# A fused attention and mixture-of-experts layer on eight cores: two instruction groups of the output-projection phase change places, and a norm's scale is computed in fewer steps

## What is computed

```python
x = x + attn(layernorm(x, eps=1e-5))            # 16 heads of 128, latent 512, S = 2048, H = 2048
x = x + ffn(layernorm(x, eps=1e-5))

def ffn(x):                                     # 8 experts, 2 of them per token, and a shared one
    h = x * rsqrt(mean(x*x) + 1e-6) * rms_weight
    probs = softmax(h @ router_w); topv, topi = top_k(probs, 2); topv /= sum(topv)
    w_dense = scatter(topi, topv)               # [tokens, 8]
    moe = sum_e w_dense[:, e] * ((silu(h @ w_gate[e]) * (h @ w_up[e])) @ w_down[e])
    return moe + (silu(h @ sw_gate) * (h @ sw_up)) @ sw_down
```

## Time and profile before

| | us |
|---|---|
| median of 2 runs | 3339.89 (3316.72 and 3363.05) |
| the profiled execution, its own time | 3065.16 |
| its span on the slowest core (core 6) | 3063.6 |
| spans of the 8 cores | 3030.8 to 3063.6 |
| mean granted TensorE clock of the 8 cores | 0.892 to 0.896 |
| output projection to router (`pb`), by the timeline | about 1045 to 1407 |
| experts (`pc`), by the timeline | about 1407 to the end |

### The profile page before, as it was taken

How to read it: one execution, slowest core, us unless ns; L and a number is a source line. 1 busy time by engine, 2 the same in 40 slices (tenths; PEclk the granted TensorE clock), 3 DMA queues, 4 the chain that set the end, 5 groups by cost and what they waited for, 6 DMA issues and landing times.

```text
span 3063.6 us, 29988 instructions; the slowest of 8 cores (3030.8 to 3063.6 us)
## 1 busy us (share of the span) xinstructions
PE 2322.3 (76%) x11593; PEld 1054.0 (34%) x11818; DVE 775.3 (25%) x1473; ACT 597.5 (20%) x905; POOL 102.6 (3%) x202
## 2 busy tenths in 40 slices
PE   0356647757777545555999999999999999999996
PEld 0122212114444322222444444444444444444443
DVE  5455362131111122111121221212122121212102
ACT  1332334217777311121000000000000000000000
POOL 1000000000000000000000000000000000000000
PEclk9977778759999767767999999999999999999998
DMA  8332000000060211016416254241634424163432
GB/s 125 136 110 69 1 0 1 0 0 1 1 111 1 84 41 42 21 35 98 71 31 105 55 84 82 46 92 28 110 55 83 83 48 90 28 110 55 83 55 110
DMA packets 48314, 182.39 MB, mean 60 GB/s; under 512 B 5656, under 2 KB 9768, under 8 KB 43056
## 3 DMA queue, kind: packets, MB, share of 16 engines
q0 software_dynamic: 40224, 130.13, 25.1%
q1 hardware_dynamic: 7952, 50.33, 4.6%
HBM read 297.93 MB, written 12.58 MB: 101 GB/s over the span
## 4 chain that ended last, share of the span: by engine, by line
PE 65%; DVE 13%; ACT 9%; issue 6%; DMA 4%; POOL 1%; DVEq 0%; ACTq 0%; SPq 0%; POOLq 0%
PE PS L1110 16%; PE PS L1064 16%; PE PS L1073 14%; ACT A_T L746 4%; PE PS L854 4%; DMA ubuf<-up_r 3%; PE PS L709 2%; DVE stats L442 2%; PE PS L609 2%; PE PS L506 2%; DVE x_lnT L484 1%; DVE ao L765 1%; ACT hT L936 1%; PE PS L737 1%; DVE sqs L638 1%
## 5 line engine op out<-in xcount | busy, mean ns | idle before, releaser
L1064 PE MATMUL PS<-hT,gbuf 128*128 128x512 bf16 x2257 | 526.4, 390 | 33.4 <-DMA ubuf<-up_r 24.5
L1110 PE MATMUL PS<-dbuf,a_fm 128*128 128x512 bf16 x2186 | 501.4, 385 | 37.6 <-DVE a_fm L1096 32.5
L1073 PE MATMUL PS<-hT,ubuf 128*128 128x512 bf16 x2186 | 490.2, 379 | 2.2
L1084 ACT ACTIVATE t1b<-PS 128x1024 f32<-128x1024 f32 x72 | 73.7, 1024 | 1472.7 <-PE PS L1078 1472.7
L1064 PEld LDWEIGHTS PS<-hT,gbuf 128*128 128x128 bf16 x2304 | 229.3, 100 | 326.6 <-issue 70.3
L1110 PEld LDWEIGHTS PS<-dbuf,a_fm 128*128 128x128 bf16 x2232 | 220.5, 99 | 308.8 <-issue 54.1
L1073 PEld LDWEIGHTS PS<-hT,ubuf 128*128 128x128 bf16 x2232 | 218.4, 98 | 263.4
L746 ACT ACTIVATE A_T<-PS,ebias 128x1024 bf16<-128x1024 f32 x256 | 272.3, 1111 | 87.1 <-PE PS L737 86.7
L1094 DVE TENSOR_TENSOR t2b<-t1b,PS 128x1024 f32<-128x1024 f32 x64 | 78.2, 1221 | 784.6 <-ACT t1b L1084 784.6
L1122 DVE TENSOR_TENSOR acc<-PS,acc 128x2048 f32<-128x2048 f32 x72 | 165.0, 2292 | 368.8 <-PE PS L1115 368.8
L709 PE MATMUL PS<-V,A_T 128*128 128x129 bf16 x1792 | 144.6, 220 | 95.3 <-ACT A_T L746 54.7
(11 more groups left out here) (201 smaller groups left out, 1414.9 us busy)
## 6 DMA issues: line engine op xcount, KB each, us to landing
gbuf<-gate_r POOLq DMA_DIRECT2D x64, 512.0 KB, 5.2
ubuf<-up_r POOLq DMA_DIRECT2D x64, 512.0 KB, 7.6
dbuf<-down_w POOLq DMA_DIRECT2D x8, 4096.0 KB, 29.4
x_in<-x_full SPq DMA_DIRECT2D x16, 1024.0 KB, 4.9
x_in<-x_own SPq DMA_DIRECT2D x8, 1024.0 KB, 5.7
WoT<-woT POOLq DMA_DIRECT2D x1, 8192.0 KB, 56.2
x_ot<-x_own SPq DMA_DIRECT2D x8, 1024.0 KB, 6.6
out<-acc SPq DMA_DIRECT2D x1, 8192.0 KB, 21.9
```

Of the source, the lines that this page charges most:

```text
L1064: e.matmul(ps_g[:, half * 512:(half + 1) * 512], gb[:, k * P:(k + 1) * P], self.hT[k][:, half * 512:(half + 1) * 512], start=(k == 0), sto ...
L1073: e.matmul(ps_g[:, 1024 + half * 512: 1024 + (half + 1) * 512], ub[:, k * P:(k + 1) * P], self.hT[k][:, half * 512:(half + 1) * 512], star ...
L1110: e.matmul(ps_d[:, nsl * 512:(nsl + 1) * 512], self.a_fm[m][:, tc * P:(tc + 1) * P], self.dbuf[:, m * H + nsl * 512: m * H + (nsl + 1) * 512],
```

## The change

Stage `a2` is cut in two. `a2` keeps the burst, the residual add and the statistics; the new `a2t` holds the scale, the shift and the writing of `h_tok`. In round `tc`, `a2(tc+1)` now stands ahead of `b1(tc)`, and `a2t(tc+1)` behind it. Only PE's list changes its order, as `b1` holds nothing but PE and ACT instructions and the ACT part of `a2` already stood behind it: PE now has the burst ahead of the transposes of `b1`. DVE and ACT keep their order, and lose the instructions named below. SP's and POOL's lists keep their order.

The waits follow: `a2(tc)` no longer waits for the evictions of `b1(tc-1)`, which now comes after it, and `b1(tc)` waits for the residual add of chunk `tc+1` (`opev[tc+1]`), since the burst has filled `PS0`.

In `a2t` both norms' scales are one: with v the variance, r = (v + 1e-5)^-0.5 and (v r^2 + 1e-6)^-0.5, the product is (v (1 + 1e-6) + 1e-11)^-0.5. It is computed as one Ln (with the bias `c_lne`) and one Exp (with the bias `c_b0`). Two ACTIVATEs and three DVE products per chunk drop out, and two memsets of 128x1 are added in `p0`.

```diff
--- before.py
+++ after.py
@@ -240,6 +240,8 @@
         self.c_pi2 = sb("c_pi2", [P, 1], F32, P0, PD)
         self.c_eps5 = sb("c_eps5", [P, 1], F32, P0, PD)
         self.c_eps6 = sb("c_eps6", [P, 1], F32, P0, PD)
+        self.c_lne = sb("c_lne", [P, 1], F32, P0, PD)
+        self.c_b0 = sb("c_b0", [P, 1], F32, P0, PD)
         self.m8 = sb("m8", [P, 8], F32, P0, PD)
         self.probs_u = sb("probs_u", [P, 8], F32, P0, PD)
         self.maskb = sb("maskb", [P, 8], F32, P0, PD)
@@ -337,6 +339,8 @@
         em(GPS, lambda e: e.memset(self.c_pi2[:, :], math.pi / 2))
         em(GPS, lambda e: e.memset(self.c_eps5[:, :], 1e-5))
         em(GPS, lambda e: e.memset(self.c_eps6[:, :], 1e-6))
+        em(GPS, lambda e: e.memset(self.c_lne[:, :], 1e-5 * 1e-6 / (1.0 + 1e-6)))
+        em(GPS, lambda e: e.memset(self.c_b0[:, :], -0.5 * math.log(1.0 + 1e-6)))
         em(GPS, lambda e: e.iota(self.rtmp[:, :], [[1, S]], base=0, channel_multiplier=0,
                                  allow_small_or_imprecise_dtypes=True))
         em(GPS, lambda e: e.iota(self.sc_c[:, :], [[1, 1]], base=0, channel_multiplier=1,
@@ -798,6 +802,7 @@
         bstage1 = {}
         bstage2 = {}
         s_h_d = {}
+        mvv = {}
         bstage = {}
 
         def stage_a1(tc):
@@ -847,7 +852,6 @@
                 wait(TEN, self.vM, aoev[tc + 1])
             if tc >= 1:
                 wait(TEN, self.vM, opev[tc - 1])
-                wait(TEN, self.sM, bstage1[tc - 1][0])
             for nsl in range(4):
                 for k in range(16):
                     em(TEN, lambda e, k=k, nsl=nsl, tc=tc:
@@ -876,22 +880,16 @@
                 self.chn(VEC, self.vM, lambda e, a0=a0, gi=gi: e.bn_stats(
                     self.stats6[:, gi * 6:(gi + 1) * 6],
                     self.acc[:, a0 + gi * 512: a0 + (gi + 1) * 512]))
-            v_mv = self.chn(VEC, self.vM, lambda e: e.bn_aggr(
+            mvv[tc] = self.chn(VEC, self.vM, lambda e: e.bn_aggr(
                 self.mv2[:, :], self.stats6[:, :].rearrange("p (g x) -> p g x", x=3)))
-            wait(SCA, self.vM, v_mv)
-            self.chn(SCA, self.sM, lambda e: e.activation(self.sc_a[:, :], self.mv2[:, 1:2], AF.Ln, bias=self.c_eps5[:, 0:1]))
-            s_r = self.chn(SCA, self.sM, lambda e: e.activation(self.sc_a[:, :], self.sc_a[:, :],
-                                                                AF.Exp, scale=-0.5))
+
+        def stage_a2t(tc):
+            a0 = tc * H
+            wait(SCA, self.vM, mvv[tc])
+            self.chn(SCA, self.sM, lambda e: e.activation(self.sc_a[:, :], self.mv2[:, 1:2], AF.Ln, bias=self.c_lne[:, 0:1]))
+            s_r = self.chn(SCA, self.sM, lambda e: e.activation(self.sc_e[:, :], self.sc_a[:, :],
+                                                                AF.Exp, scale=-0.5, bias=self.c_b0[:, 0:1]))
             wait(VEC, self.sM, s_r)
-            self.chn(VEC, self.vM, lambda e: e.tensor_mul(self.sc_c[:, :], self.sc_a[:, :], self.sc_a[:, :]))
-            v_m = self.chn(VEC, self.vM, lambda e: e.tensor_mul(self.sc_c[:, :], self.sc_c[:, :],
-                                                                self.mv2[:, 1:2]))
-            wait(SCA, self.vM, v_m)
-            self.chn(SCA, self.sM, lambda e: e.activation(self.sc_d[:, :], self.sc_c[:, :], AF.Ln, bias=self.c_eps6[:, 0:1]))
-            s_rr = self.chn(SCA, self.sM, lambda e: e.activation(self.sc_d[:, :], self.sc_d[:, :],
-                                                                 AF.Exp, scale=-0.5))
-            wait(VEC, self.sM, s_rr)
-            self.chn(VEC, self.vM, lambda e: e.tensor_mul(self.sc_e[:, :], self.sc_a[:, :], self.sc_d[:, :]))
             v_sb = self.chn(VEC, self.vM, lambda e: e.scalar_tensor_tensor(
                 self.sc_f[:, :], self.mv2[:, 0:1], -1.0, self.sc_e[:, :], ALU.mult, ALU.mult))
             wait(SCA, self.vM, v_sb)
@@ -906,9 +904,9 @@
 
         def stage_b1(tc):
             wait(TEN, self.sM, s_h_d[tc])
-            wait(TEN, self.vM, opev[tc])
-            if tc + 2 in aoev:
-                wait(TEN, self.vM, aoev[tc + 2])
+            wait(TEN, self.vM, opev[tc + 1] if tc + 1 in opev else 0)
+            if tc + 1 in aoev:
+                wait(TEN, self.vM, aoev[tc + 1])
             if tc >= 1:
                 wait(TEN, self.vM, bstage2[tc - 1][1])
                 wait(TEN, self.sM, bstage2[tc - 1][0])
@@ -981,12 +979,15 @@
         stage_a1(0)
         stage_a1(1)
         stage_a2(0)
+        stage_a2t(0)
         for tc in range(8):
             if tc + 2 < 8:
                 stage_a1(tc + 2)
+            if tc + 1 < 8:
+                stage_a2(tc + 1)
             stage_b1(tc)
             if tc + 1 < 8:
-                stage_a2(tc + 1)
+                stage_a2t(tc + 1)
             stage_b2(tc)
         self.hT_all = hT_done[7]
         self.cT_all = self.vM.n
```

## The result

| | before | after |
|---|---|---|
| median of all runs | 3063.1 us | 3022.0 us |
| median of the runs that are compared | 3061.1 us | 3019.5 us |
| ratio after to before | | 0.9864, interval 0.9849 to 0.9879 |
| profiled execution: span of the slowest core | 3063.6 us | 3020.4 us (core 5) |
| mean granted clock of the 8 cores | 0.892 to 0.896 | 0.894 to 0.902 |

The change makes the kernel 1.36% faster, 41.6 us of 3061. Forecast was a gain of 35 us and a time of 3304.9 us, between 3268 and 3342. The comparison leaves out the two runs from which the prediction took its 3339.9 us, some 9% above the other six of that kernel, and three runs of the kernel after, as long, in which the four cores of one die have a mean granted clock of 0.78 to 0.80 in place of 0.90. So the measured time, 3022.0 us, lies 246 us under the lower end of the range.

What follows compares the result with a forecast made beforehand. Rounds were bound by a chain of hand-overs, with no engine full. 7 x 4.92 = 34.4, plus 0.7 for the clock, less 0.2 for memsets, about 35 us off 3339.9: 3304.9, range 3268 to 3342.

Steps and rivals of the forecast that it cites:

- The base: Whole kernel: the gain of 35 us was taken off the median 3339.9, 275 above the profiled execution, giving 3304.9.
- The clock, ramp: Start of each burst on PE: clock at 0.50, reaching 1.00 after 5 us, taken as unchanged.
- The clock, first wave: First transposes of `b1`: may run at 2.4 GHz, gaining 0 to 0.57 us; 0.1 a round taken, 0.7 in all.
- The gap ahead of the Ln: ACT behind the evictions of `b1`: the Ln was to come 0.10 us behind the last eviction.
- The fused scale: From Ln to `h_tok`: Ln, Exp and one product take 0.95 us in place of 2.43, 1.48 less.
- The row taken for the round: One round of the earlier trace, from add to add: its links sum to 44.09 us, the whole window.
- The ends: First and last rounds: 6.75 us of `b1` moved, not saved; the gain counted as 7 x 4.92 = 34.4 us.
- A: PE's clock kept up through the shorter pause: 34 us more, 69 in all, 3271 us; chance 6%.
- B: Burst on PE never gets its clock: 90 us lost against 35 gained, 3395 us; chance 3%.
- C: Load of `ao_r` lands too late for `a1` and takes the gain back: 3340 us; chance 2%.
- D: Statistics and evictions of `b1` slow each other, only the fused scale pays: 9 us, 3331 us; chance 6%.
- E: Run spread of 1.4% hides or enlarges the gain; chance 12% over 2% faster, 4% over 2% slower, shared with other rivals.

Runs made afterwards that it cites:

- e3: The changed kernel with the transposes of `b1` also waiting for the aggregate of the statistics; ratio 0.9955 to the kernel before, round 42.32 us.
- e4: The changed kernel with four more 128x1 ACTIVATEs, one after the other, ahead of each chunk's Ln; ratio 0.9898 to the kernel before, round 39.66 us.
- e2: The kernel before with the fused scale alone, everything in its old order; ratio 0.9966 to the kernel before, round 42.67 us.
- e5: The changed kernel with 11 unread 128x512 matmuls behind the router's, while PE waits for the top two; ratio 0.9832 to the kernel before.

## Why the prediction was right and wrong

The mechanism of the gain was right: nothing overlapped in the round, the statistics went under `b1`, the experts' phase kept its length, no load came onto the path. Two numbers were wrong: the base to which the gain was applied, which put the forecast time and its whole range too high, and the size of the gain, 35 for 41, which also lies outside the 31 to 39 that the prediction gave for its mechanism alone. Link by link, for a full round, forecast and mean of 40 rounds after:

| link | forecast | after |
|---|---|---|
| add's start to `b1` | 2.72 | 2.69 |
| `b1` | 6.75 | 6.47 |
| last eviction to Ln | +0.10 | -0.16 |
| Ln to `h_tok` | 0.95 | 1.13 |
| `h_tok` to router's Exp | 2.24 | 2.24 |
| Exp to the end of the copy `cT` | 2.92 | 2.99 |
| gap and `a1` | 4.80 | 4.81 |
| gap to the burst | 0.43 | 0.43 |
| burst to the next add | 18.26 | 17.74 |
| round | 39.2 | 38.35 |

- **The base.** "The trace doesn't show where those 275 lie ... which I take to be the same there" was the step that failed: it left 275 us in the forecast time that the compared runs do not have (3061 before, 3020 after). The profiled execution, at 3065.2, was the better base: it gives 3030 for the measured 3022, and a ratio of 0.9886. That still lies just outside the interval of 0.9849 to 0.9879. The prediction saw the 9% between the profiled execution and both runs, and had no row that explained it; its range should have reached down to 3030. Its other reading of those two runs, that a change under 2% cannot be told from none, did not hold either: the interval excludes 1.
- **The clock, ramp.** "I take the ramp as unchanged": the burst is 0.46 shorter than the mean of before (18.20), and 0.52 than the one of the earlier trace rows. The largest mis-sized term. It was right that the burst does not follow the length of the pause, and wrong that the ramp is a constant: over the kernels the mean burst goes from 17.63 to 18.42, and within one from 17.05 to 18.72. That the mean of this execution fell on the short side was not foreseen, and its cause is open; this half of a microsecond a round, some 3 of the 41 us, is luck.
- **The clock, first wave.** Taken as 0.1 a round between bounds of 0 and 0.57, it gave 0.28: the wave took 0.86 on average in place of 1.14, 0.73 at best. e3 takes it away again, with the wave back at 1.14. The choice near the lower end was the error; the earlier trace rows had shown the clock at 1.00 at the very time. After the change the clock falls 2.7 to 4.4 after the add's start, and the wave starts 2.5 to 2.75 after it: where the fall comes by 2.76, the wave takes 1.14, and where it comes after 3.2, 0.73 to 0.74. Before the change it fell, in the rounds from the second add on, 2.9 to 4.0 after the add's start, so that the trace of before already held this price.
- **The gap ahead of the Ln.** Taken as 0.10 lost, it was 0.16 gained: the Ln waits for the aggregate, which ended 3 us earlier, and not for the evictions ahead of it on ACT, and it started before the last of them had ended, in all 40 rounds. The gap I took was one between instructions that wait for each other. In e4 the first of the four extra ACTIVATEs does the same, each of the others and the Ln follow the one that they wait for by 0.1, and the Ln is 1.07 behind the eviction.
- **The fused scale.** 2.54 became 1.13, not 2.43 to 0.95; 1.41 gained for 1.48 forecast. One cause is in the rows: the Exp with the bias `c_b0` takes 0.29 where the one without took 0.20, and the step "Ln, Exp and one product: 0.95" had used the old Exp. The Trainium skill ("ScalarE: Activation LUTs", What ACT_TABLE_LOAD costs) states some 93 ns for each such operand of 128x1; the trace agrees, with 0.09. The other 0.05 is in the Ln: it takes 0.34 where it starts within the last eviction, and 0.29 in e2 and e4, where it does not and the link is 1.08. The two errors, in the gap and in the scale, nearly cancel.
- **The row taken for the round.** The round of the earlier trace rows is the shortest of the five full rounds on its core, 44.09; the mean over rounds and cores is 44.25. That is 0.16 a round.
- **The ends.** "7 x 4.92" counted rounds. Measured, the two ends together gave 7.2 + 5.3 - 1.1 = 11.4 for two rounds' 9.8; they share the terms above.

Per round the terms sum: 0.16 (row) + 0.03 (gap) + 0.28 (wave) + 0.26 (Ln) - 0.18 (scale) - 0.07 (copy) + 0.52 (burst) = 1.00, for the 5.90 - 4.92 = 0.98 between measured and forecast.

Of the rivals, A (the clock is kept) did not happen: the bursts start at 0.50 still. Its mechanism exists, but it takes matmuls directly ahead of the burst, as e5's last round shows. B did not happen: no burst was over 18.73. C did not: `a1`'s first transposes followed the copy `cT` by 0.12 to 0.14 in all 40 rounds. D did not: the statistics took 3.55 beside the evictions as alone (the aggregate's end lies 5.85 behind the add's start in every kernel, before and after), and e3 priced them in full. E did not decide it: the compared runs of the kernel after lie within 0.4%, not 1.4%.

## What to carry to other kernels

When a profile shows a round whose links sum to the whole window, the gain of a reorder can be read off link by link, and it held here to 0.3 us each for everything but the clock. Look then at what stands in front of the next consumer in each engine's list, rather than at what is slow: one moved line gave 11 us more, and the cut router 27. And before a gain is put on a median, check that the profiled execution and the runs agree; where they differ by 9%, the range must hold both.

## What the runs showed of the hardware

- The time that the granted clock needs to go from 0.50 to 1.00 after a burst begins is not fixed: 2.7 to 6.0 us within one execution of the kernel after, and the burst of 68 matmuls takes 17.05 to 18.72 accordingly. It takes 15.8 if the clock is up from the start (e5, last round).
- Behind a burst the clock stays up for a while: in the kernels with nothing behind the burst it fell 2.7 to 4.4 us after the add's start. A wave of 8 transposes takes 0.73 us from first weight load to eviction if it ends before the fall, and 1.14 at the lower clock.
- Eleven matmuls of 128x512 in the pause raised the clock to 1.00 (0.91 over the first 3 us of `a1` on core 5); behind the 4.3 us of `a1` it was at 0.50 again in 39 of 40 rounds.
- An ACTIVATE that waited only for something long done (the Ln of the kernel after) started 0.16 us before the end of the one ahead of it; one that waited for the one ahead (the Exp behind it) started 0.10 behind its end.
- An ACTIVATE Exp of 128x1 takes 0.20 us without a bias operand and 0.29 with one.
